# Where the last layer's weights are rounded: from the recurrence of layer 2 to the dense experts of layer 1

## The reference, cut to what matters

```python
scale = jnp.max(jnp.abs(xb), axis=-1, keepdims=True) / 6.0
scale = jnp.maximum(scale, jnp.float32(1e-12))
xn = xb / scale
idx = jnp.searchsorted(_MID, jnp.abs(xn))
q = _GRID[idx] * jnp.sign(xn) * scale
```

## Time and profile before

| what | value |
|---|---|
| median of 3 runs | 2410.08 us (2406.3 to 2410.1) |
| the profiled execution's own time | 2409.28 us |
| its span, first to last instruction | 2407.4 us |
| layer 1's dense experts, 32 units | about 624 to 1333 us of the span |
| the recurrence | 1334 to 1454 us |
| the router of layer 2 begins | 1454.3 us |

### The profile page before, as it was taken

One profiled execution on the slowest core, in us unless ns is written; L12 is line 12 of the kernel. 1 busy time (PEld: TensorE's weight loads), 2 busy tenths in 40 slices (PEclk: granted clock), 3 DMA queues, 4 the chain that ended last, 5 costly groups with the idle time before them and its releaser, 6 DMA issues. The chain is left out here.

```text
span 2407.4 us, 33884 instructions
## 1 busy us (share of the span) xinstructions
PE 2038.5 (85%) x13199; PEld 1633.1 (68%) x13199; DVE 1376.9 (57%) x2533; ACT 981.1 (41%) x1942; POOL 284.1 (12%) x210
## 2 busy tenths in 40 slices
PE   6699699999899999999999784599936677885886
PEld 3599578888687888888888672499923564653554
DVE  3666456787765444444343694665545545544984
ACT  2244455555444544454445121244423354553222
POOL 1377000000000000000000002357610000000000
PEclk8899799999899999999999996699967857997998
DMA  2754112322022012111000100645262001001000
GB/s 80 232 157 104 41 53 88 105 88 89 1 80 72 25 36 53 35 33 39 18 1 1 47 27 14 219 112 137 36 161 78 1 19 36 18 18 38 1 9 27
DMA packets 111565, 146.14 MB, mean 61 GB/s; under 512 B 6748, under 2 KB 94731, under 8 KB 111148
## 3 DMA queue, kind: packets, MB, share of 16 engines
q1 hardware_dynamic: 101292, 130.14, 17.5%
q0 software_dynamic: 10112, 13.85, 3.3%
HBM read 121.92 MB, written 22.05 MB: 60 GB/s over the span
## 5 line engine op out<-in xcount | busy, mean ns | idle before, releaser
L1734 DVE TENSOR_TENSOR m_h_lo<-m_hf,m_h_hi 128x512 fp32r<-128x512 f32 x256 | 172.1, 690 | 355.4 <-ACT m_hf L1709 353.5
L1706 ACT ACTIVATE m_h_hi<-m_h_ps,m_bT 128x512 fp32r<-128x512 f32 x256 | 177.0, 691 | 367.0 <-PE m_h_ps L394 347.3
L639 POOL DMA_INDIRECT token_sums<-e_y,slot_row x56 | 182.4, 3258 | 107.8 <-DVE e_y L747 86.1
L1709 ACT ACTIVATE m_hf<-m_h_ps,m_bT 128x512 f32<-128x512 f32 x256 | 175.0, 684 | 0.0
L709 ACT ACTIVATE e_h_hi<-e_h_ps,e_b1T 128x320 fp32r<-128x320 f32 (+1 forms) x128 | 77.9, 609 | 167.5 <-PE e_h_ps L394 137.2
L770 DVE TENSOR_TENSOR e_h_lo<-e_hf,e_h_hi 128x320 fp32r<-128x320 f32 (+1 forms) x128 | 72.4, 583 | 112.4 <-ACT e_hf L712 112.4
L1425 DVE TENSOR_TENSOR c_h_lo<-c_hf,c_h_hi 128x512 fp32r<-128x512 f32 x120 | 82.5, 688 | 77.4 <-ACT c_hf L1381 76.2
L2059 POOL MEMSET n_bias<- 128x256 f32 x1 | 0.3, 311 | 1063.6 <-POOLq L59 1063.6
L1378 ACT ACTIVATE c_h_hi<-c_h_ps,c_b 128x512 fp32r<-128x512 f32 x88 | 62.1, 705 | 109.8 <-PE c_h_ps L394 109.2
L394 PE MATMUL m_y_ps<-m_h_hi,l_w_1hi 128*128 128x512 f32 x256 | 100.4, 392 | 3.4 <-issue 3.4
L394 PE MATMUL m_y_ps<-m_h_hi,l_w_0hi 128*128 128x512 f32 x256 | 99.7, 389 | 1.4 <-ACT m_gT L1720 1.4
(11 more groups left out here) (660 smaller groups left out, 5498.6 us busy)
## 6 DMA issues: line engine op xcount, KB each, us to landing
cT<-in_L_ffn_W_dram SPq DMA_DIRECT2D x30, 1024.0 KB
res<-in_L_cond_ew_dram SPq DMA_DIRECT2D x22, 1024.0 KB, 5.1
cT<-in_L_ffn_w_dram SPq DMA_DIRECT2D x16, 1024.0 KB, 4.9
res<-gates_rows SPq DMA_DIRECT2D x8, 1024.0 KB, 9.1
l_mod<-modulation_rows SPq DMA_DIRECT2D x16, 512.0 KB, 6.6
token_rows<-d_tok SPq DMA_DIRECT2D x2, 2112.0 KB, 10.9
token_sums<-res SPq DMA_DIRECT2D x2, 2048.0 KB, 7.5
res<-token_sums SPq DMA_DIRECT2D x8, 512.0 KB, 7.6
```

Of the source, the lines that this page charges most:

```text
L639: pool.indirect_dma_start(out=sums, out_offset=bass.IndirectOffsetOnAxis(ap=st.slot_row[0:r, e, j:j + 1], axis=0), in_=y[0:r, e % 2, j, :] ...
L1706: act.activation(hs[0][:, f, :], h_ps[:, f % HB, :], ACT.Relu, bias=bT[:, at:at + 1])
L1709: act.activation(hf[:, f % HB, :], h_ps[:, f % HB, :], ACT.Relu, bias=bT[:, at:at + 1]).then_inc(act_done, 1)
L1734: dve.tensor_tensor(hs[1][:, f, :], hf[:, f % HB, :], hs[0][:, f, :].bitcast(F32), ALU.subtract).then_inc(h_ready, 1)
```

## The change

The class `QuantWeights` now lives in layer 1's dense experts and only rounds. A new class, `TurnWeights`, lives in the recurrence and only turns.

- GpSimd, idle before, waits in `l1_ffn_phase` for `mix_used` to reach 1 and then does three passes: it loads a third of the weights into `yk` (its queue's direct DMAs, 704 KB), waits until the pass is rounded, stores it to DRAM as it lies, and waits for the store.
- VectorE rounds a pass in 4 pieces of 7 portions each, one portion after each `f` of a unit, so 28 portions a pass. `ROUND_FROM` starts the passes at units 10, 17 and 24. A piece is 24 blocks of 16 (128x384; 22 blocks in the last pass).
- In the recurrence SyncE loads the rounded weights with two DMAs in place of five; TensorE turns one 128x128 tile a step from step 10 on (34 tiles), ScalarE evicts the 10 groups, and SyncE stores the result and waits for it within this block. VectorE does only its own transposition. No work of the turning is left after the last step.
- The router's SyncE no longer waits for the stores.

```diff
-        @block.vector (of l2_cond_phase)
-            pieces = rounding.pieces(dve)
             for s in range(S):
                 dve.wait_ge(tanhed, s + 1)
                 dve.transpose(dst[:, :, :, s], h[:, s % 2, :].rearrange("p (j c) -> p j c", c=C)).then_inc(kept, 1)
-                if s >= rounding.FIRST_STEP:
-                    next(pieces, None)
-            for _ in pieces:
-                pass
             dve.wait_ge(kept, S)
...
+    ROUND_FROM = (2 * NB + 2, 4 * NB + 1, 6 * NB)
+        rounding = QuantWeights(sem, yk[:, :, :, :].rearrange("p a c n -> p (a c n)"), *later)
+        @block.gpsimd
+        def _(pool):
+            pool.wait_ge(mix_used, 1)
+            for i in range(rounding.PASSES):
+                rounding.load(pool, i)
+                rounding.store(pool, i)
...
                     if e + 1 < E8 and ((b == 2 and u > NB) or u == NB - 1):
                         prepare_second_layer(e + 1, f)
+                    if f == 0 and u in ROUND_FROM:
+                        pieces = rounding.pieces(dve, ROUND_FROM.index(u))
+                    if u >= ROUND_FROM[0]:
+                        next(pieces, None)
...
+    def store(self, pool, i):          # QuantWeights
+        pool.wait_ge(self.rounded, (i + 1) * self.PIECES)
+            ... direct DMAs of the pass to kept_gu or kept_dn
+        pool.wait_ge(stored, self.in_count(i))
+    def pieces(self, dve, i):          # one yield = one portion
+        dve.wait_ge(self.w_in[i], self.in_count(i))
+        for n in range(self.PIECES):
+            link(dve.tensor_reduce(scale, x, AX.X, ALU.max, apply_absolute_value=True))
+            yield
+            link(dve.tensor_scalar(scale, scale, 1.0 / 6.0, 1e-12, ALU.mult, ALU.max))
+            link(dve.reciprocal(inv, scale))
+            yield
+            link(dve.scalar_tensor_tensor(out=x, in0=x, scalar=BELOW, in1=bc(inv, 2, QB), op0=ALU.mult, op1=ALU.mult))
+            yield
+            link(dve.tensor_scalar(m.bitcast(U32), x.bitcast(U32), EXPONENT, None, ALU.bitwise_and))
+            link(dve.tensor_scalar(m, m, 1.0, GRID, ALU.max, ALU.mult))
+            yield
+            link(dve.tensor_tensor(x, x, m, ALU.add))
+            yield
+            link(dve.tensor_tensor(x, x, m, ALU.subtract))
+            yield
+            dve.tensor_tensor(x, x, bc(scale, 2, QB), ALU.mult).then_inc(self.rounded, 1)
+            dve.wait_ge(self.rounded, i * self.PIECES + n + 1)
+            yield
...
+class TurnWeights:
+    FIRST_STEP = 10
+    def load(self, sp):
+        sp.dma_start(self.gu[:, :, :].rearrange("p j k -> p (j k)"), self.kept_gu).then_inc(self.gu_in, 16)
+        sp.dma_start(self.dn[:, :, :].rearrange("p c i -> p (c i)"), self.kept_dn).then_inc(self.dn_in, 16)
```

More of the change, by code:

```diff
@@ L1013, in _ @@
             r.load(sp, W, None)
-            rounding.wait_stored(sp)
         @block.gpsimd
@@ L1922, in load @@
     def load(self, sp):
[L1923 to L1962, removed]
@@ L1964, in turns @@
-    def turns(self):
[L1966 to L1973, removed]
-    def turn_steps(self, pe, st):
[L1977 to L1983, removed]
+        sp.dma_start(self.gu[:, :, :].rearrange("p j k -> p (j k)"), self.kept_gu).then_inc(self.gu_in, 16)
@@ L1984, in turn_steps @@
+        sp.dma_start(self.dn[:, :, :].rearrange("p c i -> p (c i)"), self.kept_dn).then_inc(self.dn_in, 16)
+    def turns(self):
+        groups = [("gu", c, j, min(j + 4, GT)) for c in range(KC) for j in range(0, GT, 4)]
+        return groups + [("dn", c, j, min(j + 4, HC)) for c in range(KC) for j in range(0, HC, 4)]
+    def turn_steps(self, pe, st):
+        for n, (what, c, lo, hi) in enumerate(self.turns()):
+            pe.wait_ge(self.gu_in if what == "gu" else self.dn_in, 16)
             if n >= self.BANKS:
@@ L1995, in turn_steps @@
                 yield
-                step += 1
     def keep_steps(self, act):
[L2000 to L2005, removed]
+        for n, (what, c, lo, hi) in enumerate(self.turns()):
             for j in range(lo, hi):
                 yield
-                step += 1
             act.wait_ge(self.turned, n + 1)
@@ L2039, in l2_cond_phase @@
         sums = mem.enter_context(nc.psum_tensor("n2_sums", [P, 2, BLK], F32))
-        rounding.open_banks(nc, mem)
+        turning = TurnWeights(nc, sem, mem, kept_gu, kept_dn, turned_gu, turned_dn)
+        turning.open_banks(nc, mem)
         w_in, bias_set, bias_in = sem("n2_w_in"), sem("n2_bias_set"), sem("n2_bias_in")
@@ L2053, in _ @@
             sp.dma_start(bias[0:1, :], b.unsqueeze(0)).then_inc(bias_in, 16)
-            rounding.load(sp)
-            rounding.store(sp)
+            turning.load(sp)
+            turning.store(sp)
         @block.gpsimd
@@ L2060, in _ @@
             pool.memset(ones[:, :], 1.0).then_inc(bias_set, 1)
-            rounding.clear(pool)
+            turning.clear(pool)
         @block.tensor
@@ L2085, in _ @@
             inputs(0)
-            turn_steps = rounding.turn_steps(pe, st)
+            turn_steps = turning.turn_steps(pe, st)
             for s in range(S):
@@ L2092, in _ @@
                     inputs(s + 1)
-                if s >= rounding.FIRST_STEP:
+                if s >= turning.FIRST_STEP:
                     next(turn_steps, None)
-            for _ in turn_steps:
-                pass
         @block.scalar
         def _(act):
-            keep_steps = rounding.keep_steps(act)
+            keep_steps = turning.keep_steps(act)
             for s in range(S):
@@ L2103, in _ @@
                 act.activation(h[:, s % 2, :], sums[:, s % 2, 0:KC * C], ACT.Tanh).then_inc(tanhed, 1)
-                if s >= rounding.FIRST_STEP:
+                if s >= turning.FIRST_STEP:
                     next(keep_steps, None)
-            for _ in keep_steps:
-                pass
         @block.vector
         def _(dve):
-            pieces = rounding.pieces(dve)
             for s in range(S):
@@ L3274, in _, with l1_phases @@
                 add(p)
-def l1_phases(nc, sem, st, a, back, shared):
+def l1_phases(nc, sem, st, a, back, shared, later):
     with ExitStack() as mem:
@@ L3336, in adaln_ffn_4_layers @@
         sem.layer_end()
-        l3_ffn_phases(nc, sem, st, spare, st.res, out, kept_gu, kept_dn)
+        l3_ffn_phases(nc, sem, st, spare, st.res, out, turned_gu, turned_dn)
         sem.stack.close()
```

93 lines of the change are left out of this document (66 added, 27 removed).

## The result

| | before | after |
|---|---|---|
| median of 11 runs | 2409.84 us (2406.3 to 2413.1) | 2393.51 us (2391.39 to 2403.59) |
| ratio of the runs, 95% interval | | 0.9942 (0.9930 to 0.9953), that is -14.0 us (-16.9 to -11.3) |
| span of the profiled execution | 2407.4 us | 2390.5 us |
| predicted | | 2397.7 us, range 2393 to 2404 |

What follows compares the result with a forecast made beforehand. It took VectorE's rounding portions to set the recurrence's pace, and TensorE to bound the dense experts. Terms -10.9 - 1.5 + 0 = -12.4 us gave 2396.9 against the profiled execution, 2397.7 against the median; range 2393 to 2404.

Steps and rivals of the forecast that it cites:

- the pitch: Recurrence: without VectorE's portions a step takes 1.58 us (bounds 1.55 to 1.63) against 1.765; 59 steps give -10.9 us.
- the block end: End of the recurrence: no turning or stores follow the last transposition, so the router's GpSimd block starts earlier, -1.5 us.
- step 4's gap: Recurrence start: TensorE's 1.23 us stand for its own instructions behind the loads, kept at 0 change; could be -1.2 or +1.5.
- The turned tiles: Recurrence: 34 tiles on TensorE lie in its wait for the transposition, 0.00 to 0.05 us a step; 3.4 us if cover vanished.
- rival 1: Recurrence: TensorE bounds the turning steps, 34 steps keep 1.765 us and only 25 gain, so 2404 us; chance 0.12.
- The sign that was named: Recurrence end: GpSimd's first router instruction would come 1.2 to 1.5 us behind the last transposition if the forecast was right.
- The dense experts: Rounding on VectorE is hidden behind a full TensorE: 0 us, or +5 at the slow rows' durations.
- rival 2: Dense experts: rounding runs at the slow durations and delays TensorE, +5 us, so 2402.7; chance 0.07.
- `h_low(5)` of unit 17: Dense experts: VectorE finishes it at 1019.6, TensorE wants it at 1021.3; this 1.7 us is the smallest spare.
- GpSimd's passes: Dense experts: each pass's store and load take under 60 us with 10 us landing each, so hidden, 0 us.
- rival 3: Dense experts: a late pass stops VectorE and so TensorE; at 90 us each costs 26 us, 2424; chance 0.03.
- the 77 us: Dense experts: time from a pass's end to the next start, within which GpSimd's store and load must finish.

Runs made afterwards that it cites:

- run 3: Kernel before, with VectorE's rounding portions left out of the recurrence, loads and turning kept: 2393.9 us, ratio 0.9939.
- run 2: Kernel after, without TensorE's 34 turned tiles and ScalarE's 10 evictions, weights stored untransposed: 2394.4 us, ratio 0.9945.
- run 5: Kernel after, whose recurrence loads raw weights with the kernel before's five short-row DMAs in place of two: 2396.5 us, ratio 0.9936.
- run 1: Kernel after, without GpSimd's three passes and VectorE's 84 rounding portions in the dense experts: 2393.7 us, ratio 0.9939.
- run 6: Kernel after, with one more 128x384 VectorE operation in each of the 84 portions in the dense experts: 2401.7 us, ratio 0.9958.
- run 4: Kernel before with all its work, but TensorE's recurrence loads read and VectorE's transposition writes 32 adjacent columns (values differ): 2376.8 us, ratio 0.9869.
- run 7: Kernel after, output kept: in the recurrence VectorE copies inputs and transposes the state into contiguous buffers that TensorE reads: 2379.0 us, ratio 0.9870.
- run 9: Kernel after, with TensorE reading and the transposition writing 32 adjacent columns in the recurrence (regrouped tokens): 2379.2 us, ratio 0.9870.
- run 10: Kernel after, with adjacent columns only for the 8 weight loads of `inputs` (wrong tokens): 2386.8 us, ratio 0.9909.
- run 11: Kernel after, with adjacent columns only for `recur` and the transposition, `inputs` left strided: 2377.2 us, ratio 0.9859.
- run 8: Kernel of run 7, with GpSimd building the router's `r_same` during the recurrence in place of at the router's start: 2373.0 us, ratio 0.9832.

## Why the prediction was right, step by step

The mechanisms held. The terms that were off were all off to the same side (2.6 us at the pitch, 0.8 at the block end, 1.35 at step 4's gap), less 0.3 us lost in all the rest, which is how the spans come to differ by 16.9 us and not by 12.4. The prediction had named just these three for its lower end.

- **The pitch** (-10.9 forecast, -13.5 measured). The mechanism was right: run 3 has the gain without the move. The 1.536 us measured lie outside its bounds of 1.55 to 1.63. The term was mis-sized in the gap between two tanhs, 1.21 taken and 1.17 found; 59 times 0.04 is 2.4 us, and the rest is rounding and a tanh of 366 ns in place of 370. The row of 1.25 us was a step with a VectorE portion; the added time was the portion's, not the tile's, since run 3 keeps the tiles without the portions and has a median gap of 1.17. The free step alone had the right number.
- **The turned tiles** at 0: right, run 2, and rival 1 falls. The cover was called thinner; it is thick enough at 1.54.
- **The block end** (-1.5 forecast, -2.3 measured). The row of the bare block end was badly chosen: between the dense experts and the recurrence stands one more block, in which GpSimd clears the layer's semaphores. A bare end is 0.5 us, the one with it 1.3 to 1.4. The sign that was named, 1.2 to 1.5 us behind the last transposition, was therefore not seen.
- **The start**: step 4's gap was kept at 0 change, bound -1.2; it went away in the profiled execution (-1.35). That is chance as far as run 5 shows. Half a microsecond more ahead of the first transposition, and 0.3 in the stages before, went the other way.
- **The dense experts** at 0: right, runs 1 and 6. The portion prices held to 0.01 us (0.56 forecast and 0.55 measured for 128x384, 0.36 for the masks), so rival 2, the slow durations, falls. `h_low(5)` of unit 17 was forecast to end 13.4 us behind the unit's first; it did at 13.2. The timeline of VectorE in the kernel after, in that unit:

```profile
1006.50 0.69 DVE L1742 TENSOR_TENSOR m_h_lo<-m_hf,m_h_hi 128x512 fp32r<-128x512 f32 x1 [11.55 <-ACT m_hf L1717]
1007.11 0.55 DVE L1966 TENSOR_REDUCE m_yk<-m_yk 128x24 f32<-128x384 f32 x1
...
1008.54 1.41 DVE L1774 SCALAR_TENSOR_TENSOR m_yg<-m_y_ps,m_b2T,res 128x512 f32<-128x512 f32 x2
...
1013.54 0.55 DVE L1971 SCALAR_TENSOR_TENSOR m_yk<-m_yk 128x384 f32<-128x384 f32 x1
...
1018.98 0.69 DVE L1742 TENSOR_TENSOR m_h_lo<-m_hf,m_h_hi 128x512 fp32r<-128x512 f32 x1
```

- **GpSimd's passes** were in time, so rival 3 falls, with one surprise. Timeline of GpSimd in the kernel after, then of VectorE during the second store:

```profile
929.75 0.58 POOL L1946 DMA_DIRECT2D rounded_gate_up<-m_yk  x1 [188.65 <-DVE m_yk L1980]
...
934.90 0.54 POOL L1932 DMA_DIRECT2D m_yk<-in_L_ffn_w_up_dram  x1 [4.01 <-DMA rounded_gate_up<-m_yk]
...
1079.80 0.56 POOL L1949 DMA_DIRECT2D rounded_gate_up<-m_yk  x1 [143.47 <-DVE m_yk L1980]
...
1095.93 0.72 POOL L1935 DMA_DIRECT2D m_yk<-in_L_ffn_w_down_dram  x1 [14.99 <-DMA rounded_gate_up<-m_yk]
...
1079.54 2.50 DVE L1742 TENSOR_TENSOR m_h_lo<-m_hf,m_h_hi 128x512 fp32r<-128x512 f32 x4
1093.54 0.69 DVE L1742 TENSOR_TENSOR m_h_lo<-m_hf,m_h_hi 128x512 fp32r<-128x512 f32 x1 [11.51 <-ACT m_hf L1717]
```

The store of the first pass came back 4 us after its last issue, that of the second 15 us after, where the prediction had allowed 10; both far inside the 77 us. In the second case SyncE's 1 MB broadcast of the gates, issued at 1076.55, went through the same DMA engines at that moment; that it made the difference is likely and not shown, since no run moves it. The prediction's rival was that VectorE blocks GpSimd. The Trainium skill's box on VectorE blocking such DMAs (SBUF — State Buffer, "SBUF: two separate sides") says that GpSimd can't write their descriptors while VectorE runs a two-port mode. The 15 us can't come from that: VectorE stood idle for 11.51 of them. The issues took 0.54 to 0.99 us, that of 1079.80 beside a busy VectorE 0.56, and no run here shows that block.

## What to carry to other kernels

When an engine looks like the bound of a loop, ask first why its instructions take what they take: the add that took 1.31 us where its size says 0.53 was the real finding of the profile before, and the prediction used it only as a bound. Moving the work away gained 14 us; reading adjacent columns gained 32 with the work left in place (run 4, which computes something else), and both together 31 (run 7, with the result kept, and run 9). The two do not add. A walk through one period with the durations of rows tells the spare of a full stage well enough to be spent (1.7 us forecast, run 6); and after every such gain look at which of the remaining waits, here TensorE's stops without a releaser and `r_same`, is next.

## What the runs showed of the hardware

- Weight loads of TensorE that read 32 columns 256 bytes apart took 235 to 242 ns against 110 to 121 for adjacent ones (runs 4, 10, 11), and while they ran other engines' instructions with adjacent operands grew: VectorE's 128x352 add from 482 to 1,308 ns, ScalarE's tanh from 224 to 370. The Trainium skill says that TensorE, ScalarE and VectorE's own pair never wait for each other (SBUF — State Buffer, "SBUF: two separate sides"). The runs differ from it where a stride of 256 bytes is involved, most plainly in the tanh (223 ns in run 10, 392 in run 11); which part of the memory is shared they do not tell. VectorE's own strided write and read of 64 elements (run 7) did no such harm: the tanh took 223 ns and the loads 112 to 116 beside them.
- In a loop of 1.06 us TensorE stops again and again without a releaser: 7.8 us in 64 steps (run 7), 9.2 (run 8), 6.1 (run 9), against single stops of at most 1.2 us at 1.54. That it waits for instructions is the likeliest reading, not shown.
- The scatter of the shorter kernels (up to 12 us, in runs with and without the passes) has at least one source in layer 3: the profiled execution of run 9 needed 10.8 us more there and had a lower granted clock there. The spread of runs fits: the fastest seven of the kernel after (up to 2394.0 us) had a mean granted clock of 0.907 to 0.909, the slowest three (2399.7 to 2403.6) 0.905, 0.905 and 0.903. Run 6 does not fit (0.906 to 0.909, its longest execution at 0.908). What makes the chip grant a clock, and which is cause and which effect, was not settled.
